# Edge gate finished on ScalarE, and the edge pipeline one step deeper behind the running sums

## What is computed

```python
h = relu(layernorm(x))                                   # every node
em = relu(layer_norm(concat(h[src], h[dst]) @ msg_w + msg_b) * msg_g + msg_beta) * edge_weight
messages = segment_sum(em, dst) / count(dst)             # 0 where a node has no edge
gate = sigmoid(h @ gate_w + gate_b)                      # one number per node
h_new = relu(layer_norm(concat(h, messages) @ upd_w + upd_b) * upd_g + upd_beta)
out = x + gate * h_new + (1 - gate) * h
```

## Time and profile before

| | us |
|---|---|
| median of 3 runs | 1020.86 (1020.46 to 1021.62) |
| the profiled execution: time | 1019.86 |
| its span in the profile | 1017.1 |

### The profile page before, as it was taken

How to read it: one execution, slowest core, us unless ns; L and a number is a source line. 1 busy time by engine, 2 the same in 40 slices (tenths; PEclk the granted TensorE clock), 3 DMA queues, 4 the chain that set the end, 5 groups by cost and what they waited for, 6 DMA issues and landing times.

```text
span 1017.1 us, 20909 instructions
## 1 busy us (share of the span) xinstructions
PE 705.2 (69%) x3696; PEld 547.4 (54%) x3696; DVE 945.0 (93%) x4103; ACT 875.1 (86%) x3664; POOL 680.7 (67%) x602
## 2 busy tenths in 40 slices
PE   1877776777777777777477767676867676666740
PEld 1555554555555555555366556565656565555530
DVE  6999999999999999999869999998998999999990
ACT  2899999999999999999778988888788897888860
POOL 5788888888888888100344777776776777677564
PEclk9999996555555555555578998989798989999975
DMA  4255555555555455332121222221212122121110
GB/s 142 79 153 149 154 152 151 151 154 151 149 155 153 148 153 155 113 115 82 52 82 59 62 73 65 68 70 58 68 61 70 56 68 70 55 68 60 55 58 21
DMA packets 56028, 100.65 MB, mean 99 GB/s; under 512 B 13728, under 2 KB 15600, under 8 KB 55948
## 3 DMA queue, kind: packets, MB, share of 16 engines
q1 hardware_dynamic: 35766, 64.54, 17.6%
q0 software_dynamic: 18912, 34.84, 14.4%
q10 hardware_dynamic: 1270, 0.53, 0.3%
HBM read 52.34 MB, written 51.45 MB: 102 GB/s over the span
## 4 chain that ended last, share of the span: by engine, by line
DVE 56%; issue 18%; ACT 12%; PE 4%; DVEq 4%; POOL 3%; DMA 1%; ACTq 0%; SPq 0%; POOLq 0%
DVE work L430 11%; DVE st L344 9%; DVE work L441 8%; ACT junk L393 5%; DVE work L447 5%; DVE acc L441 5%; DVE acc L885 4%; PE pa L1056 3%; POOL out L557 3%; DVE mv L350 3%; DVE work L452 2%; DVEq L109 1%; DVE gt L423 1%; DVE omg L426 1%; ACT hrow L386 1%
## 5 line engine op out<-in xcount | busy, mean ns | idle before, releaser
L552 POOL DMA_INDIRECT ring<-in_x,src_i x196 | 228.7, 1167 | 175.8 <-ACT hrow L386 110.1
L552 POOL DMA_INDIRECT ring<-in_x,gidx x196 | 237.7, 1213 | 59.7 <-issue 59.7
L557 POOL DMA_INDIRECT out<-work,sidx x196 | 209.8, 1071 | 88.5 <-issue 56.9
L1056 PE MATMUL pt<-ident,hrow 128*128 128x128 f32 x588 | 143.4, 391 | 116.8 <-ACT hrow L386 108.5
L1093 PE MATMUL py<-w_u,work 128*128 128x129 f32 x784 | 203.8, 441 | 0.0
L409 ACT ACTIVATE work<-work,gt 128x128 f32<-128x128 f32 x589 | 199.6, 403 | 2.6 <-DVE work L447 2.6
L1093 PEld LDWEIGHTS py<-w_u,work 128*128 128x128 f32 x784 | 174.9, 328 | 40.4 <-issue 40.4
L1056 PEld LDWEIGHTS pt<-ident,hrow 128*128 128x128 f32 x588 | 96.6, 197 | 145.9 <-ACT hrow L386 136.6
L386 ACT ACTIVATE hrow<-xload,nb,rs 128x128 f32<-128x128 f32 x392 | 161.6, 484 | 14.4 <-DVE nb L379 7.5
L441 DVE SCALAR_TENSOR_TENSOR work<-py,rs,g_upd 128x128 f32<-128x128 f32 x588 | 163.4, 339 | 4.2 <-ACT rs L373 4.2
L393 ACT ACTIVATE junk<-py 128x128 bf16<-128x128 f32 x588 | 150.5, 266 | 8.7 <-PE py L1131 7.8
(11 more groups left out here) (151 smaller groups left out, 1543.4 us busy)
## 6 DMA issues: line engine op xcount, KB each, us to landing
xload<-in_x SPq DMA_DIRECT2D x98, 256.0 KB, 3.3
out<-work SPq DMA_DIRECT2D x98, 256.0 KB, 2.0
running_sums<-acc SPq DMA_DIRECT2D x49, 256.0 KB
ring<-in_x,src_i POOLq DMA_INDIRECT x196, 3.2
ring<-in_x,gidx POOLq DMA_INDIRECT x196, 3.2
out<-work,sidx POOLq DMA_INDIRECT x196, 2.3
w_all<-in_L_gnn_msg_w ACTq DMA_DIRECT2D x1, 128.0 KB
w_all<-in_L_gnn_upd_w ACTq DMA_DIRECT2D x1, 128.0 KB
```

The source lines that it names most:

```text
L552: pool.indirect_dma_start(out=dest, out_offset=None, in_=rows, in_offset=bass.IndirectOffsetOnAxis(ap=idx, axis=0), **(if_tail if rows is ...
L557: pool.indirect_dma_start(out=out, out_offset=bass.IndirectOffsetOnAxis(ap=idx, axis=0), in_=rows, in_offset=None, **if_tail).then_inc(s, 16)
L1056: last = nc.tensor.transpose(dest[:, k * H:(k + 1) * H], rows[:, k, :], ident[:, :])
```

## The change

In the edge stage the flip of the sums, the copy `at` and the product `py` work on group s-5 and not s-4; post, gate, relu and final of a group come one step later too. TensorE makes the flip of the sums first in its step. ScalarE copies `at` right behind `ht_dst`, and waits ahead of `ht_dst` of s-2 for the `py` of s-6, whose slot it overwrites. The gate 1/(1+ge) is made on ScalarE, as exp(-ln(1+ge)), by two operations of `gates`; VectorE makes only `omg` = 1 - gate of them (stage "rest"). VectorE scales `t_buf` ahead of the second statistics, and no longer at the end of the step. In the node stage the final addition is that of s-6 at the end of the step. The refills are dealt out over 36 groups. The diff, with its context cut:

```diff
@@ -52,7 +52,7 @@
...
 AHEAD = 8
-REFILLED = 40
+REFILLED = 36
 EPS = 1e-5
...
@@ -307,6 +307,8 @@
...
                              "cw": 1,
+                             "gate": 2,
+                             "rest": 1,
                              "msgw": 1,
...
@@ -400,6 +402,17 @@
...
                                                              scale=-1.0))
+
+        def gates(act, g, which):
+
+            L, b = ed["gate"], g.at % 4
+            if which == 0:
+                ed["post"].after(act, g)
+                L.begin(act, g)
+                L.mark(nc.scalar.activation(e1[:, b, :], ge[:, g.at % 2, :], ACT.Ln, bias=1.0))
+            else:
+                L.wait()
+                L.mark(nc.scalar.activation(gt[:, b, :], e1[:, b, :], ACT.Exp, scale=-1.0))
 
...
@@ -646,9 +659,6 @@
...
                     minus_mean(dve, nd, s.back(1), G)
-                f = s.back(7)
-                if live(f, NG):
-                    final(dve, nc.vector, nd, f, o[:, f.at % 4])
                 if new:
...
@@ -669,6 +679,9 @@
...
                     beta(dve, nd, g, t_buf[:, g.at % 4], be_upd)
+                f = s.back(6)
+                if live(f, NG):
+                    final(dve, nc.vector, nd, f, o[:, f.at % 4])
 
...
@@ -823,7 +836,7 @@
...
             def edge_step(s):
-                g, m = s.back(6), s.back(4)
+                g, m = s.back(7), s.back(4)
                 fin, new, summing = live(g, EG), live(s, EG), live(m, EG)
...
@@ -831,21 +844,17 @@
...
                 if fin:
-                    gain(dve, ed, g, 0)
+                    ed["gate"].after(dve, g)
+                    one_mark(ed["rest"], dve, g, nc.vector.tensor_scalar(omg[:, g.at % 4, :], gt[:, g.at % 4, :], -1.0, 1.0,
+                                                                         ALU.mult, ALU.add))
                 if new:
...
                     L = ed["stats"]
-                    row_stats(L, s, slot(s, 0, at)[:, 0:2], 0)
-                if fin:
-                    gain(dve, ed, g, 1)
-                if new:
-                    row_stats(L, s, slot(s, 0, at)[:, 2:4], 2)
-                if fin:
-                    gain(dve, ed, g, 2)
+                    row_stats(L, s, slot(s, 0, at), 0)
                 if live(s.back(1), EG):
                     minus_mean(dve, ed, s.back(1), 2 * G, -0.5)
-                f = s.back(8)
+                f = s.back(9)
                 if live(f, EG):
...
@@ -855,6 +864,14 @@
...
                     beta(dve, ed, q, acc[:, q.at % 4], be_msg, G, "beta_m", "gamma_m")
+                if fin:
+                    if beyond(g, 4):
+                        dve.wait_ge(s_scat[g.at % 4], g.rounds(16 * G))
+                    else:
+                        dve.wait_ge(s_st[g.at], 16 * len(range(g.at, NG, 4)))
+                    ed["rstd"].after(dve, s)
+                    one_mark(ed["gamma"], dve, g, by_std(t_buf[:, g.at % 4], py[:, g.at % 2], s.at % 4, 3 * G, g_upd))
+                    beta(dve, ed, g, t_buf[:, g.at % 4], be_upd)
                 if new:
...
@@ -867,11 +884,7 @@
...
                 if fin:
-                    if beyond(g, 4):
-                        dve.wait_ge(s_scat[g.at % 4], g.rounds(16 * G))
-                    else:
-                        dve.wait_ge(s_st[g.at], 16 * len(range(g.at, NG, 4)))
-                    ed["gain"].after(dve, g)
+                    ed["rest"].after(dve, g)
                     fat = slot_base(dve, g)
...
@@ -895,13 +908,8 @@
...
                     moment(L, s, 2 * G, 2)
-                if fin:
-                    ed["rstd"].after(dve, s)
-                    one_mark(ed["gamma"], dve, g, by_std(t_buf[:, g.at % 4], py[:, g.at % 2], s.at % 4, 3 * G, g_upd))
-                if fin:
-                    beta(dve, ed, g, t_buf[:, g.at % 4], be_upd)
-
-            run_steps(dve, node_step, NG, 7, 9, 8, first=4, beside=edge_step)
+
+            run_steps(dve, node_step, NG, 6, 9, 8, first=4, beside=edge_step)
 
...
@@ -920,7 +928,7 @@
...
 
-            run_steps(dve, edge_step, EG, 8, 2 * EUN, EUN, first=7, beside=tail_step)
+            run_steps(dve, edge_step, EG, 9, 2 * EUN, EUN, first=6, beside=tail_step)
 
...
@@ -983,8 +991,8 @@
...
                     ed["stats"].after(act, s.back(1))
-                if live(s.back(6), EG):
-                    ed["post"].after(act, s.back(6))
+                if live(s.back(7), EG):
+                    ed["post"].after(act, s.back(7))
                 if live(s.back(3), EG):
...
@@ -994,11 +1002,17 @@
...
                 if live(g, EG):
+                    if beyond(g, 4):
+                        ed["upd"].after(act, g.back(4))
                     one_mark(ed["ht"], act, g, nc.scalar.activation(ht_dst[:, (g.at + NG) % 4, :], pt[:, 1, :], ACT.Copy))
-                if live(s.back(7), EG):
-                    gated_relu(act, ed, s.back(7))
-                if live(s.back(5), EG):
-                    post(act, ed, s.back(5), (s.at + 1) % 4, 3 * G, G, 1.0)
+                g = s.back(5)
+                if live(g, EG):
+                    evacuate(ed, g, at_[:, g.at % 2, :], pa[:, :], ACT.Copy, "at", "aflip")
+                if live(s.back(8), EG):
+                    ed["gate"].after(act, s.back(8))
+                    gated_relu(act, ed, s.back(8))
+                if live(s.back(6), EG):
+                    post(act, ed, s.back(6), (s.at + 1) % 4, 3 * G, G, 1.0)
                 g = s.back(1)
...
@@ -1006,11 +1020,12 @@
...
                     H_.mark(h_rows(g, hrow[:, (g.at + NG) % 4], slot(g, 0, at), 0))
+                if live(s.back(6), EG):
+                    gates(act, s.back(6), 0)
                 if live(g, EG):
                     H_.mark(h_rows(g, h_dst[:, (g.at + NG) % XS], slot(g, 1, at), G))
-                g = s.back(4)
-                if live(g, EG):
-                    evacuate(ed, g, at_[:, g.at % 2, :], pa[:, :], ACT.Copy, "at", "aflip")
+                if live(s.back(6), EG):
+                    gates(act, s.back(6), 1)
                 if live(s.back(2), EG):
...
@@ -1035,7 +1050,7 @@
...
 
-            run_steps(act, edge_step, EG, 7, 2 * EUN, EUN, first=6, beside=tail_step)
+            run_steps(act, edge_step, EG, 8, 2 * EUN, EUN, first=6, beside=tail_step)
 
...
@@ -1095,6 +1110,10 @@
...
             def edge_step(s):
+                g = s.back(5)
+                if live(g, EG):
+                    ed["sum"].after(pe, g)
+                    one_mark(ed["aflip"], pe, g, flip(pa[:, :], acc[:, g.at % 4]))
                 g = s.back(2)
...
@@ -1107,16 +1126,12 @@
...
                     one_mark(ed["msg"], pe, g, last)
-                g = s.back(4)
-                if live(g, EG):
-                    ed["sum"].after(pe, g)
-                    one_mark(ed["aflip"], pe, g, flip(pa[:, :], acc[:, g.at % 4]))
                 g = s.back(1)
...
                     one_mark(ed["flip"], pe, g, flip(pt[:, 1, :], h_dst[:, (g.at + NG) % XS]))
-                g = s.back(4)
+                g = s.back(5)
                 if live(g, EG):
...
@@ -1137,7 +1152,7 @@
...
             run_steps(pe, node_step, NG, 2, 9, 8, first=2, beside=edge_step)
-            run_steps(pe, edge_step, EG, 4, 2 * EUN, EUN, first=2)
+            run_steps(pe, edge_step, EG, 5, 2 * EUN, EUN, first=2)
 
...
```

## The result

| kernel | median us | against the kernel before, same chip |
|---|---|---|
| before | 1021.1 (1020.5 to 1021.6) | |
| after | 1121.9 (1121.1 to 1122.1) | ratio 1.0986, 95% interval 1.0967 to 1.1005 |

The change makes the kernel 9.9% slower. The profiled execution has a span of 1119.6 us, against 1017.1.

The account below looks back on a forecast made before the run. A closed VectorE-TensorE-ScalarE ring was taken to bound the edge step at 9.50 us. With the new step at 11.2, 42 x (11.2 - 9.5) = 71.4 us, with the drain 77, added to 1019.9 gives 1097, median 1098; range 1040 to 1140.

Parts of the forecast that it names:

- The ring of before and what leaves it: Edge stage: closed ring over VectorE, TensorE and ScalarE, 9.50 us a step; `at` would no longer wait for same-step sums.
- The new ring at full clock: Edge stage: ScalarE's `ht` waits for TensorE's `py`, behind flips awaiting ScalarE's last `h_dst` row; 10.0 us a step at 2.4 GHz.
- the logarithm: ScalarE's new gate operation between the `h` rows in the edge step: 0.15 us, bounds 0.05 and 0.3.
- The clock: TensorE in the edge stage: one low stretch each step, 1.2 us, making the step 11.2 us; bounds 10.0 and 13.1.
- The page on the clock gate: Trainium skill section, cited for TensorE: a long enough idle wait drops the clock, so each step's burst starts low.
- The drain: End of the kernel: 26 GpSimd operations behind the last awaited final, before 22; +5.4 us, bounds 0 and +9.
- The node stage: Node steps on VectorE, final moved to the step's end: taken as 0, with a possible gain of 12 us.
- GpSimd and VectorE: Edge stage: GpSimd's 9.4 us a step hidden by any longer ring; VectorE's own work about 9.0 us.
- What would show it: Trace signs: ScalarE idle before `ht`, TensorE some 3 us before `pt`, `nb` waiting 1 to 2 us, edge clock under 0.9.
- the clock falls as seldom as before: Rival, edge stage: same ring, with low clock costing only 0.2 us a step; 10.2 us a step, 1056 us; chance 0.25.
- The clock stays low altogether: Rival, edge stage: TensorE at 1.2 GHz throughout, 13.1 us a step, 1178 us; chance 0.05.
- The new wait never comes last: Rival, `ht` on ScalarE: `py` of s-6 is done before ScalarE arrives; 1022 us, or 1010 with node gain; chance 0.13.

## Why the prediction was right, point by point

- **The ring of before and what leaves it**: right. The wait of `at` for the sums is gone in after.
- **The new ring at full clock, 10.0 us**: right to 0.05 us. With the clock kept up it is 9.96. By terms: start of the flips 0.05 (0.05 said); `at` to the end of `h_dst` 5.99 at any clock (0.49 + 2.22 + 1.54 + 0.15 + 1.65 = 6.05 said); the logarithm 0.10 (805.60 to 805.70; 0.15 said).
- **The clock**: the mechanism right, the size too small. This is the term that failed. I took one low stretch a step at 1.2 us, as in the earlier trace rows, with 3.1 us for a whole step at 1.2 GHz as the upper end. The runs show 12.37 - 10.07 = 2.3 us in the mean. The stretch in the rows of before had begun ahead of the flips and ended in the middle of `py`; in after the shown one reaches over both flips and all of `py` (6.25 us instead of 3.35, 2.9 more), though not in every step. This is the term that makes 1098 too low: 42 x (2.3 - 1.2) = 46 us. Against it stands the step of before, which I took at 9.50 from one round, where the 40 steps have a mean of 9.79: the ring at full clock adds 10.07 - 9.79 = 0.28 us and not 0.5, 9 us less over 42 steps. (Most of the 0.29 between 9.50 and 9.79 are the three turns of the loop.) Together 71 + 46 - 9 = 108, and 107.0 is what the stretch from the first to the 49th `nb` shows.
- **The page on the clock gate**: the Trainium skill, "TensorE: Matmul & The Clock Gate", section "HAM oscillation — how this bites in real kernels", describes bursts that each start cold after an idle wait. The trace agrees: after the 3.44 us gap TensorE starts at 1.2 GHz, the granted clock is 0.79, and with the gap filled it is 1.00. On this kernel the waits are for another engine, not for a DMA as in the page's example. I should have given it more weight than the single price of the earlier trace rows.
- **The drain**: +9.9 us behind the last `nb`, 5.4 said. The unbroken run of scatters behind the last wait for VectorE has 26 operations, as said, and 22 in before:

```profile
1073.31 0.98 POOL L570 DMA_INDIRECT out<-work,sidx  x1 [2.86 <-DVE work L465]
...
1107.95 0.98 POOL L570 DMA_INDIRECT out<-ring,tidx  x1 [0.31 <-issue]
```

  From the first start to the last it is 34.6 us, 28.5 in before, so 6.1 of the 9.9 us are in this run, 5.4 for the four more and the rest because each takes 1.39 us and not 1.36. The other 4 lie ahead of it, among edge steps in the same ring; I didn't follow them further.
- **The node stage**: said 0 with a bound of -12; it is -14.5 up to the first edge `nb`, and 12 us by the part alone. The bound named the right place and the right size, and I took the other end of it. Whether the cause is the final's waits, as the bound supposed, isn't shown.
- **GpSimd and VectorE**: right that they are hidden (GpSimd waits for VectorE in 38 steps).
- **What would show it**: as said, ScalarE idle before `ht`, TensorE idle before `pt` (3.5 us), a clock under 0.9. VectorE's wait comes in two pieces, before `omg` for ScalarE's gate (1.4 us) and before `nb` (1.4 us); the first I had put at 0.2 at most. I take both to lie in slack, since the ring of ScalarE and TensorE is the longer one; this wasn't tried alone.
- **The rivals**: "the clock falls as seldom as before" (1056) is refuted by the granted clock, 0.79 against 0.89, and the step of 12.37 us. "The clock stays low altogether" (1178, a step of 13.1) is refuted by `pm`, which runs at full clock (0.39) in the shown step. "The new wait never comes last" is refuted by 39 waits; and its time of 1022 for an open ring, 1010 with the node stage's gain, was too good as well, for opening it with `py` first gives 1030: another ring through TensorE stands at 10.2 us in the mean.
- **Slips in the sums**: 1.9 + 4.1 + 1.06 is 3.2 us more than 3.9 and not 3.1, and 1140 us stands for a step of 12.2 us and not 12.3. Nothing hangs on either.

The 24 us between 1098 and 1122, by the profiled spans: edge steps +107.0 where 71 was said, drain +9.9 where 5 was said, node stage -14.5 where 0 was said; +102.4 together where 77 was said. (The medians differ by 100.8.) That the forecast is off by 24 us and not by 40 is luck: the node stage's gain, taken as 0, stands against what the edge steps and the drain cost more.

## What to carry to other kernels

When a step is made deeper to break one wait, write down what each in-order queue has in front of the instruction that frees the reused buffer: here ScalarE waits for TensorE's last product, which stands behind transposes that wait for ScalarE's last rows, and the two engines take turns. Ask of each such ring how much TensorE work it holds, for here the ring created the idle gap after which the clock was at 1.2 GHz, and then paid for it. And try the parts of a change alone: one harmless-looking line in another stage was worth 1.1%, hidden under a loss of 10%.

## What the hardware showed that I had not expected

- Twelve useless matmuls a step (2.8 us of TensorE time each step) made the kernel 92 us faster, by raising the granted clock of the edge stage from 0.79 to 1.00.
- Moving the 128x512 addition from behind `nb` to the end of VectorE's node step takes the step from 4.74 to 4.60 us, in some 90 steps of an engine without a gap, though no instruction was saved. The cause is open.
- The same kernel takes 1020 us on some chips and 1420 on others. The traces from the slower ones have more idle time, with the releasers "issue" and "remote" in two stretches, up to about 360 us and from about 760 us on, and in both GpSimd issues indirect DMAs; in the node steps between them the step is as long as on the other chips (4.60 us in the new order). Why these chips differ isn't shown.
